# Queries of two batches in one pass in the first three layers of a six-layer transformer, with all engine queues ordered anew

## What is computed

```python
def _L0_xattn_ref(input_tensor, ctx_tensor, ctx_att_mask, Wq, bq, ...):
    q = _split_heads(input_tensor @ Wq.T + bq)
    k = _split_heads(ctx_tensor @ Wk.T + bk)
    v = _split_heads(ctx_tensor @ Wv.T + bv)
    scores = jnp.einsum('bqhd,bkhd->bhqk', q, k) * scale
    ...
    probs = jax.nn.softmax(scores, axis=-1)
    ctx = jnp.einsum('bhqk,bkhd->bqhd', probs, v)
    h = ctx @ Wo.T + bo
    y = h + input_tensor
    ...
    return (y - mu) * jax.lax.rsqrt(var + LN_EPS) * ln_g + ln_b
x = _L0_xattn_ref(x, ctx_1024, mask, ...)
x = _L1_xattn_ref(x, ctx_1024, ctx_1024, ...)
x = _L2_xattn_ref(ctx_1024, x, ...)   # SELF, CROSS and FFN
x = _L3_xattn_ref(x, ctx_1024, ...)
```

## Time and profile before

| | us |
|---|---|
| median of 3 runs | 1284.87 (1284.42 to 1285.02) |
| profiled execution | 1283.64 |
| its span, first to last instruction | 1281.7 |
| PE busy in it | 1214.8 |
| DVE busy | 1037.5 |
| ACT busy | 796.0 |
| POOL busy | 742.6 |
| granted TensorE clock, mean | 0.994 of full |

### The profile page before, as it was taken

How to read it: one execution, slowest core, us unless ns; L and a number is a source line. 1 busy time by engine, 2 the same in 40 slices (tenths; PEclk the granted TensorE clock), 3 DMA queues, 4 the chain that set the end, 5 groups by cost and what they waited for, 6 DMA issues and landing times.

```text
span 1281.7 us, 42264 instructions
## 1 busy us (share of the span) xinstructions
PE 1214.8 (95%) x18380; PEld 991.5 (77%) x18380; DVE 1037.5 (81%) x1781; ACT 796.0 (62%) x1257; POOL 742.6 (58%) x879
## 2 busy tenths in 40 slices
...
GB/s 228 120 26 43 18 35 18 20 41 10 26 31 9 3 19 4 2 6 24 3 3 3 10 26 2 23 51 20 9 9 9 26 1 1 10 17 18 67 3 66
DMA packets 16079, 33.90 MB, mean 26 GB/s; under 512 B 2039, under 2 KB 6423, under 8 KB 15895
## 3 DMA queue, kind: packets, MB, share of 16 engines
...
...
## 4 chain that ended last, share of the span: by engine, by line
PE 55%; DVE 24%; POOL 9%; issue 5%; ACT 4%; DMA 1%; POOLq 0%; SPq 0%; DVEq 0%; ACTq 0%
DVE s_nm L1534 9%; PE ps L1212 7%; PE ps L1227 7%; PE ps L1200 6%; PE ps L1144 6%; PE ps L1181 5%; PE ps L1029 5%; PE ps L1082 4%; PE ps L1041 3%; DVE s_KH L1488 3%; PE ps L1054 3%; DVE s_Os L1541 2%; PE ps L1178 2%; POOL s_xs L1722 2%; DVE s_stt L1581 2%
## 5 line engine op out<-in xcount | busy, mean ns | idle before, releaser
L1534 DVE TENSOR_REDUCE s_nm<-ps 128x8 fp32r<-128x960 f32 (+1 forms) x352 | 398.2, 1161 | 43.7 <-PE ps L1082 25.4
L1378 ACT ACTIVATE s_PU<-ps 120x1024 f32<-120x1024 f32 (+1 forms) x288 | 282.1, 1023 | 116.3 <-PE ps L1159 115.1
L1144 PE MATMUL ps<-s_Qs,s_KH 32*120 32x256 f32 (+2 forms) x4608 | 191.7, 288 | 11.9 <-DVE s_Os L1541 4.2
L1144 PEld LDWEIGHTS ps<-s_Qs,s_KH 32*120 32x120 f32 (+1 forms) x4608 | 154.2, 179 | 41.5 <-issue 17.7
L1730 POOL TENSOR_TENSOR s_Os<-s_Os,s_Rc 128x512 f32<-128x512 f32 x80 | 86.9, 1086 | 169.3 <-DVE s_Rc L1549 163.9
L1181 PE MATMUL ps<-s_PU,s_Vp 120*32 120x256 f32 x2048 | 136.5, 387 | 7.8 <-DVE s_nm L1534 2.9
L1082 PE MATMUL ps<-s_KH,s_Qs 32*128 32x240 f32 x3072 | 128.8, 292 | 11.5 <-DVE s_nm L1534 3.4
L1669 POOL TENSOR_TENSOR s_xs<-s_xs,s_rowv 128x512 f32<-128x512 f32 x96 | 127.6, 1329 | 12.1 <-DMA s_xs<-x_nat 1.0
L1200 PE MATMUL ps<-s_W,s_oT 128*128 128x256 f32 x896 | 126.6, 290 | 7.7 <-POOL s_oT L1690 4.8
L1029 PE MATMUL ps<-s_xT,s_W 128*128 128x256 f32 (+1 forms) x736 | 126.4, 317 | 3.4 <-POOL s_xT L1677 1.8
L1082 PEld LDWEIGHTS ps<-s_KH,s_Qs 32*128 32x128 f32 x3072 | 103.5, 186 | 31.7 <-issue 9.2
...
## 6 DMA issues: line engine op xcount, KB each, us to landing
...
s_mi<-mask SPq DMA_DIRECT2D x8, 3.8 KB
...
```

Of the source, the lines that this page charges most:

```text
L1144: t = e.matmul(banks[j][0:n, wide * x:wide * x + wide], kz[row[j], lk, g, c, k0:k0 + n], q[row[j], lq, g, qs_], start=(x == 0 and y_ == 0) ...
L1378: t = e.activation(P_of(i, k)[0:n, :, :], pair("B", i, k)[0:n, :, :], ACT.Exp, scale=0.25)
L1534: e.tensor_reduce(o, v, AX.X, ALU.max, negate=True).then_inc(sem["max"])
```

## The change

`TWOS` now names all six layers. In L0, L1 and SELF a pair of batches therefore shares one buffer of `s_xT`, `T`, `Th` and `Tl` come in two halves for a pair (L1, SELF), `Th` and `Xl` of L0 take two loaded batches, and `Q`, `Qh`, `Ql` are two steps of a pair, each a half of the weights' columns for both batches. In L1, `bo` waits for both halves of `T`. The tables `WANT` and `AT` are new for every step and every load, and a few assumed lengths are others.

```diff
-TWOS = ("CROSS", "FFN", "L3")
+TWOS = ("L0", "L1", "SELF", "CROSS", "FFN", "L3")
...
-    ("xT", "L0"): (1.41, 4.88, 7.98, 13.99, 22.22, 25.14, 28.49, 31.41, 52.55, 55.65, 76.5, 79.42, 95.13, 108.91, 119.24, 142.74),
...
-LAND = 1.8
-MOVED = dict(xT=.65, cT=.6, mi=.15, ws=.65, row=1.5, x=1.35, msk=.6, cst=.4, mci=.4, out=.65)
+LAND = 1.3
+MOVED = dict(xT=1.0, cT=.95, mi=.3, ws=1.0, row=1.6, x=1.35, msk=.6, cst=.4, mci=.6, out=.65)
...
-                add("POOL", "bo", after=[("T", pair, 0), ("row", nr, 0)])
+                add("POOL", "bo", after=[("T", pair, f) for f in parts] + [("row", nr, 0)])
...
-                add("DVE", "Kl", after=[("Kh", i, 0)])
+                add("DVE", "Kl", long=2.0 if layer == "L1" else None, after=[("Kh", i, 0)])
...
-        p.stages["Qh", i, 0].after.append(("cst", 0, 0))
+        p.stages["Qh", even(i), 0].after.append(("cst", 0, 0))
...
-                    w.wait_ge(sem["T"], nth("T", even(i)))
+                    w.wait_ge(sem["T"], max(nth("T", even(i), f) for f in halves(i)))
```

More of the change, by code:

```diff
@@ new lines @@
+    ("rec", "SELF"): (453.75, 470.04, 491.52, 503.13, 523.45, 542.26, 558.98, 587.47, 599.76, 617.13, 636.88, 659.97, 672.96, 690.57, 714.23, 728.98),
+    ("nmul", "SELF"): (454.35, 470.87, 491.92, 503.53, 523.85, 546.21, 566.31, 587.87, 607.22, 617.53, 645.55, 660.78, 673.36, 693.18, 715.56, 729.38),
+    ("turn", "SELF"): (455.86, 473.21, 494.76, 505.1, 525.04, 548.7, 575.53, 589.06, 611.26, 627.53, 650.98, 674.34, 686.44, 694.93, 718.55, 731.9),
+    ("OTh", "SELF"): (457.16, 475.93, 495.59, 507.51, 525.98, 549.53, 580.47, 592.69, 612.92, 628.36, 657.35, 675.17, 687.7, 695.76, 720.16, 733.77),
@@ new lines @@
+    ("OTl", "SELF"): (458.8, 477.86, 496.28, 515.16, 526.8, 555.76, 581.16, 600.01, 617.38, 633.58, 660.22, 675.86, 690.82, 700.7, 726.35, 735.4),
[29 rows of a table added]
+    ("max", "CROSS"): (717.49, 722.39, 740.19, 750.71, 756.4, 773.66, 785.75, 796.41, 810.78, 820.57, 833.12, 845.4, 864.02, 873, 881.61, 898.54, 719.23, 720.34, 741.26,
+        748.71, 757.46, 774.72, 787.07, 797.73, 812.42, 822.25, 834.81, 846.46, 865.16, 870.09, 882.68, 897.47, 724.52, 727.15, 743.88, 760.24, 766.6, 781.01, 793.56,
+        798.8, 819.17, 823.96, 840.35, 854.88, 867.47, 876.67, 890.47, 901.07, 723.46, 729.23, 744.95, 761.64, 765.53, 779.94, 792.49, 799.87, 818.11, 827.05, 838.61,
+        853.82, 866.41, 875.61, 891.53, 902.14),
@@ new lines @@
+    ("M", "CROSS"): (727.71, 734.31, 750.68, 763.87, 769.29, 787.73, 799.4, 807.33, 823.66, 831.46, 845.1, 856.31, 868.69, 880.01, 896.07, 903.35),
+    ("mTe", "CROSS"): (728.44, 735.16, 751.82, 765.1, 769.93, 788.26, 800.12, 808.04, 824.37, 833.21, 845.81, 856.83, 871.42, 880.9, 896.6, 904.41),
[4 rows of a table added]
+    ("exp", "CROSS"): (731.95, 741.52, 754.95, 767.08, 777.46, 791.04, 802.98, 813.81, 828.88, 836.13, 851.01, 858.27, 873.19, 882.88, 898.71, 907.41, 732.86, 742.43,
[7 rows of a table added]
+    ("rec", "CROSS"): (743.37, 761.39, 768.74, 786.82, 797.48, 814.13, 820.24, 832.38, 843.8, 857.53, 871.15, 886.85, 897.02, 913.07, 927.51, 937.06),
@@ new lines @@
+    ("nmul", "CROSS"): (743.77, 761.79, 769.14, 787.22, 801.2, 814.53, 820.69, 836.58, 844.39, 857.93, 873.02, 887.25, 897.42, 913.66, 937.8, 944.29),
+    ("turn", "CROSS"): (747.84, 763.92, 770.33, 794.62, 802.39, 815.72, 825.02, 839.67, 848.13, 859.12, 874.73, 888.95, 899.6, 915.12, 938.99, 955.71),
+    ("OTh", "CROSS"): (748.67, 765.37, 772.16, 797.74, 804.8, 818.6, 832.69, 840.5, 849.58, 862.15, 879.47, 890.52, 908.32, 926.96, 946.51, 956.54),
+    ("OTl", "CROSS"): (749.36, 766.06, 773.53, 798.43, 805.49, 819.29, 833.38, 841.19, 850.27, 862.84, 880.16, 891.7, 909.01, 929, 950.14, 957.88),
[88 rows of a table added]
@@ new lines @@
+    ("x", 6, 0): 32.68, ("x", 7, 0): 33.15, ("row", 1, 0): 123.22, ("row", 2, 0): 289.58, ("row", 3, 0): 553.73, ("row", 4, 0): 886.35, ("row", 5, 0): 953.35,
[19 rows of a table added]
+}
+LONG = dict(mci=.5, msk=.95, cst=.47, xT=.47, cT=.47, mi=.47, ws=.47, row=.47, x=.47, out=.47, bo=1.45, N=.98, Xl=1.4, K=1.345, K0=.7, Kh=1.18, Kl=1.6, V=1.415, Ve=.64, Ch=.5, Cl=1.37,
+            mf=.4, mc=.1, A=0.68, max=1.065, M=.225, mTe=.27, B=0.71, D=0.232, exp=.91, PV=0.863, X=.62, rec=.25, nmul=1.22, turn=.68, OTh=.52, OTl=.8, O=1.42, y=.6, st=.93, rs=1.8,
+            ln=.98, lng=2.85, F1=1.28, T=.44, Th=.48, Tl=.58, Q=1.42, Qh=.72, Ql=.77, Fa=.57, Fv=.67, Hl=2.53, F2=2.97, wb=.81, Wd=.65, wa=.08, wg=.8, Wh=.52, Wl=1.43, qs=.57, qm=.1, qa=.6, qw=1.25)
```

33 lines of the change are left out of this document (6 added, 27 removed), and 584 rows, old and new, of tables (AT, WANT).

## The result

The changed kernel takes 1294.72 us (median of 4 runs, 1290.87 to 1296.15) against 1284.92 before (1284.42 to 1285.02): ratio 1.0072, interval 1.0054 to 1.009. It is slower by 0.7%. The forecast was 1281.3, the range 1273 to 1290. The prediction was wrong.

A forecast was written before the change was run, and what follows sets the result against it. TensorE was taken to bound L0 and SELF, VectorE L1. The terms -0.9 - 1.7 + 1.0 - 2.0 = -3.6 us took the profiled 1283.64 to 1280.0; 1.23 up to the median gave 1281.3, range 1273 to 1290.

The forecast's parts named there:

- Part 1: Query matmuls of L0, L1, SELF: 576 become 288, twice as wide; 1.3 us of TensorE's work, -0.9 us counted.
- Part 2: Query evictions on VectorE, fewer and wider: 0.24 us a pair, counted in L1's 8 pairs, -1.7 us.
- Part 4: New order of all queues: about half of 4.3 us of TensorE's waits for s_Qs and s_xT goes, -2.0 us.
- That it is half rests on no row: The prediction's own caution on its order term of -2.0 us, which it called the weakest.
- Part 3: Start with its loads: W0's copy behind the second turned x delays loads; +1.0 us, ends -1.2 and +4.2.
- The row on SP: Sign in the start: SP's weight load that went at 8.78 goes at about 11.0, waiting for W0's landing buffer.
- the first D: Sign in the start: at 24.90 before, it would come at about 29.1, +4.2 us.
- The 3.2 us are only moved: Start: two query steps of 1.6 us no longer precede the third batch's first scores, offsetting the 4.2 us slip.
- the upper end of +4.2: Worst case for the start: the slip of the first D with nothing taken back.
- I take nothing from L3's tail: End of L3: the last 40 steps of PE are the same in both orders, so 0 us was counted.
- The lock step in L1: Rival: TensorE waits 1.2 us for a turned x at each of L1's 8 pairs, +9.6, 1292.9; slower had 0.21.

The follow-up runs named there:

- b_w0late: The kernel before with one fault put in: on ScalarE the copies of W0 and W2 stand behind the second batch's x; median 3.9 us up.
- after_again: The changed kernel once more, unaltered, for a second profile; its span is 5.4 us longer than the first profile's.
- a_split: Changed kernel with L0's turned x copied and landing buffers freed batch by batch, start's steps spread out, stores in result order; 1282.4 us, 0.15% under the kernel before.

## Why the prediction was wrong

**Part 1, matmuls: right in kind, sized low.** A half's step takes 35.59 - 34.10 = 1.49 us in the changed kernel. TensorE was busy for 1214.2 us, up to 6.8 of that for the clock; before 1214.8 and 5.1: 2.3 us less work, where 1.3 was forecast. The rule of the Trainium skill ("TensorE: Matmul & The Clock Gate", section "The mechanism"), that a weight load overlaps matmuls in flight only when the row group differs, would by an estimate with the page's time for a load have given some 31. The traces do not agree with it here: the prediction was right to follow the rows.

**Part 2, evictions: right in size.** The line that was to show it:

```profile
L1495 DVE SCALAR_TENSOR_TENSOR s_Qs<-ps,s_cst,s_Qs 128x512 fp32r<-128x512 f32 x80 | 58.2, 735 | 26.6 <-ACT s_Qs L1343 26.2
```

58.2 for 80, forecast 59, against 64.2 in the earlier trace rows. PE's idle time from 240 to 440 fell from 14.2 to 10.8, but that window cuts both kernels at different work. Between the steps of keys it fell from 21.9 to 20.3 in L1 and SELF together: 1.6 us, near the 1.7 forecast, though nothing here separates it from what the order did.

**Part 4, the order: its -2.0 did not come.** Parts 1, 2 and 4 were to bring 4.6 us. From the mark to CROSS's keys the changed kernel took 616.4 us, the kernel before 622.6, of which 1.7 is clock. The 4.5 left look like the 4.6, by luck: 1.9 of them are work that only moved ahead of the mark, and the other 2.6 are less work of TensorE. Waiting, which parts 2 and 4 were to shorten by 3.7, is as long as before (25.3 and 25.4): the 1.6 less in L1 and SELF are given back between the mark and L1's keys (5.1 us, before 3.4). "That it is half rests on no row" was said.

**Part 3, the start: the step that failed.** The row on SP was right (11.95, forecast "about 11.0"), and so was the first D: 29.68, forecast 29.1. The error is the sentence "The 3.2 us are only moved, but they fill the waits that the slip makes: 4.2 less 3.2 leaves +1.0", and the upper end of +4.2. It stopped at the second pair. The third batch's first scores came at 51.45, 9.3 us late, and by the mark the start had cost some 12 us, not 1.0. Three things were left out. The prediction saw that the copy of the fourth batch's x stands ahead of the turned maxima, but not that the third pair's copies stand ahead of the exponentials, 6.5 us of waits more. It put down no price for the clock, which fell to half at such a wait: up to 5.1 us. And it let slack take back what b_w0late shows to stay whole over 1200 us.

**The sentence "I take nothing from L3's tail": the second failure.** TensorE's last 40 rows are the same, but the stores are SyncE's. +2.2.

**The spread.** The profiled execution was a lucky one: the clock fell at neither of the waits in CROSS and at L3's begin, where after_again lost most of its 5.4 us. The prediction had nothing on that. The clock of the changed kernel was 0.986 to 0.992 (mean of eight executions 0.989), before 0.989 to 0.996 (mean 0.993), and a_split, with the same order of TensorE and a repaired start, had 0.990 to 0.997 (mean 0.993). The difference, 0.004 of 1290 us, is 5 us, about what the stretches in the start take (5.1 and 6.8 us in its two profiles). That the rest of the run has more falls than before is not shown.

**The rivals.** The lock step in L1 (1292.9, nearly the time that came) did not happen: L1 and SELF got shorter. It happened in the start, through two landing buffers freed together, a mechanism that was named for the wrong layer.
